# Filling TensorE's waits with products of the identity that nothing reads, in a two-layer perceiver block

## The reference, cut to what matters

```python
x = x + xattn0(layernorm(x), ctx)        # 16 heads, 4096 keys, relative bias
x = x + ssm(layernorm(x))                # projection in, convolution, selective scan, gate, projection out
x = x + mix(layernorm(x))                # token shift, r = sigmoid(xr Wr), k = relu(xk Wk)^2, r * (k Wv)
x = x + xattn1(layernorm(x), ctx, mask)  # 16 heads, 4096 keys, masked
x = x + tm(layernorm(x))                 # v, r, decay scan over time, projection out
x = x + ffn(layernorm(x))                # gate, up, down with rounded weights and activations
```

## Time and profile before

| | us |
|---|---|
| median of 3 runs | 1400.04 (1394.95, 1400.04, 1403.46) |
| the profiled execution | 1400.61 |
| its span in the trace | 1398.7 |
| PE busy | 1245.5 (89%) |
| DVE busy | 1027.9 (73%) |
| ACT busy | 928.2 (66%) |
| POOL busy | 203.0 (15%) |
| mean granted clock of TensorE | 0.929 |

### The profile page before, as it was taken

One profiled execution on the slowest core, in us unless ns is written; L12 is line 12 of the kernel. 1 busy time (PEld: TensorE's weight loads), 2 busy tenths in 40 slices (PEclk: granted clock), 3 DMA queues, 4 the chain that ended last, 5 costly groups with the idle time before them and its releaser, 6 DMA issues.

```text
span 1398.7 us, 25689 instructions
## 1 busy us (share of the span) xinstructions
PE 1245.5 (89%) x8951; PEld 647.6 (46%) x8952; DVE 1027.9 (73%) x2295; ACT 928.2 (66%) x1203; POOL 203.0 (15%) x183
## 2 busy tenths in 40 slices
PE   7759989999999999789998629999999999999746
PEld 4436634544454446345555411445445445445423
DVE  4217889999999971469999439878778787781666
ACT  2316757667767776356675181799999999999614
POOL 2212200000000000059996040000000000000000
PEclk9979989999999999999999765899999999999875
DMA  4898885455455310117776856134434344300000
GB/s 154 211 240 265 260 224 116 93 130 115 93 122 113 73 45 20 68 57 248 259 248 218 221 83 139 32 74 81 87 69 93 69 86 80 75 2 23 1 0 15
DMA packets 100684, 160.97 MB, mean 115 GB/s; under 512 B 8497, under 2 KB 57137, under 8 KB 100065
## 3 DMA queue, kind: packets, MB, share of 16 engines
q1 hardware_dynamic: 99088, 158.13, 46.1%
q10 hardware_dynamic: 1488, 1.42, 0.4%
HBM read 114.34 MB, written 45.18 MB: 114 GB/s over the span
## 4 chain that ended last, share of the span: by engine, by line
PE 64%; DVE 12%; issue 11%; ACT 5%; DMA 2%; SPq 2%; POOL 1%; DVEq 1%; POOLq 0%; ACTq 0%
PE PS L546 17%; PE PS L501 16%; PE PS L533 15%; PE PS L525 4%; PE PS L274 3%; PE PS L283 2%; DMA Pz<-in_ctxT 2%; ACT Pz L668 2%; DVE Vz L1068 2%; DVE OT L1076 2%; DVE Kz L1068 1%; PE PS L799 1%; ACT Pz L666 1%; SPq L262 1%; PE PS L858 1%
## 5 line engine op out<-in xcount | busy, mean ns | idle before, releaser
L668 ACT ACTIVATE Pz<-PS 128x1024 f32<-128x1024 f32 x488 | 483.5, 1018 | 125.8 <-PE PS L533 123.2
L589 DVE CUSTOM_DVE_ANT_0 Pz<-PS,Tz 128x512 bf16<-128x512 f32 x512 | 334.4, 689 | 88.4 <-PE PS L501 84.3
L501 PE MATMUL PS<-Kz,Qz 96*128 96x512 bf16 x1024 | 366.0, 401 | 32.3 <-issue 22.0
L533 PE MATMUL PS<-Qz,Kz 99*128 99x256 bf16 x2048 | 310.7, 274 | 4.7 <-ACT Pz L666 3.0
L586 DVE TENSOR_REDUCE mx<-PS 128x1 f32<-128x512 f32 x448 | 289.6, 686 | 14.2 <-PE PS L501 13.5
L546 PE MATMUL PS<-Pz,Vz 128*17 128x256 f32 x4096 | 272.4, 384 | 0.2 <-ACT Pz L668 0.2
L533 PEld LDWEIGHTS PS<-Qz,Kz 99*128 99x128 bf16 x2048 | 195.3, 98 | 124.9 <-ACT Pz L666 10.4
L501 PEld LDWEIGHTS PS<-Kz,Qz 96*128 96x128 bf16 x1024 | 99.5, 98 | 197.3 <-DVE mx L589 77.8
L546 PEld LDWEIGHTS PS<-Pz,Vz 128*17 128x17 f32 x4096 | 94.2, 97 | 133.0 <-issue 61.2
L672 ACT ACTIVATE PS<-Tz 128x512 f32<-128x512 bf16 x240 | 144.3, 601 | 7.6
L525 PE MATMUL PS<-Tz,identb 128*128 128x512 bf16 x272 | 105.0, 386 | 4.1 <-ACT Pz L668 3.9
(11 more groups left out here) (218 smaller groups left out, 1209.4 us busy)
## 6 DMA issues: line engine op xcount, KB each, us to landing
k_parts<-Pz SPq DMA_DIRECT2D x192, 128.0 KB
Kz<-k_parts SPq DMA_DIRECT2D x64, 384.0 KB, 4.8
v_ones<-Pz SPq DMA_DIRECT2D x32, 544.0 KB, 5.1
Vz<-v_ones SPq DMA_DIRECT2D x64, 272.0 KB, 6.0
Pz<-in_ctxT SPq DMA_DIRECT2D x32, 512.0 KB, 5.9
Kz<-k_parts SPq DMA_DIRECT2D x64, 256.0 KB, 5.5
Kz<-k_parts SPq DMA_DIRECT2D x64, 128.0 KB, 5.9
Kz<-in_mask_pieces SPq DMA_DIRECT2D x16, 512.0 KB, 5.8
```

The lines of the kernel that those rows point to most:

```text
L501: e.matmul(PS[:, unit_bank(k, u) if bank is None else bank, :], Qz[0:ROWS, o:o + 128], Kz[b][0:ROWS, hh, c * CH:c * CH + CH], start=True, ...
L533: m = e.matmul(PS[:, bank, o:o + T], Kz[b][0:KROWS, hh, i * 128:i * 128 + 128], Qz[0:KROWS, q:q + T], start=(L == 0), stop=True, skip_grou ...
L589: e.tensor_tensor_reduce(junk[:, u % 3, :], ps, masks[:, tt, c * CH:c * CH + CH], 1.0, LOWEST, ALU.add, ALU.max, to).then_inc(sem("at_seen ...
L668: m = e.activation(probs(i), PS[:, 2 * (i % 2):2 * (i % 2) + 2, :].rearrange("p a n -> p (a n)"), ACT.Exp)
```

## The change

A helper puts `n` products of the bf16 identity with itself (four times side by side, 512 columns) into one PSUM bank. Calls of it are put behind and between TensorE's work in the layer norms but the first, in `fin_pe`, behind the output projection of the state space step (with a wait for the value copies out of bank 6 ahead of it), in the mixing, in the fourth part and in the feed-forward's down part. No other engine's list changes, and no existing product, wait or increment.

```diff
+        def keep_busy(e, n, bank=6):
+            for _ in range(n):
+                e.matmul(PS[:, bank, :].rearrange("p (a n) -> p a n", n=128), identb[:, :],
+                         identb[:, :].unsqueeze(1).broadcast_to([128, 4, 128]), start=True, stop=True,
+                         skip_group_check=True)
 def ln_pe(e, k):
                     m = e.transpose(PS[:, c, r * 128:r * 128 + 128], xn[:, r, c * 128:c * 128 + 128], identf[:, :])
+                    if k and c == 0 and r < RT - 1:
+                        keep_busy(e, 1)
                 m.then_inc(sem("ln_tps"), 1)
+            if k:
+                keep_busy(e, 5)
 def fin_pe(e, L):
             fin_pe_sums(e, L, 4)
+            keep_busy(e, 3)
             fin_pe_spread(e, L, 4)
+            keep_busy(e, 4)
             for r in range(RT // 2, RT):
                 fin_pe_rows(e, L, NG - 1, r)
+            keep_busy(e, 14)
 def ssm_pe(e):
             proj_pe(e, lambda m_, r: yg[:, m_, r * 128:r * 128 + 128], wout, DC)
+            e.wait_ge(sem("kv_vcopied"), 8 * NCH + 2)
+            keep_busy(e, 16)
 def mix_pe(e):
             e.wait_ge(sem("ld_mix"), 16 * 4)
+            keep_busy(e, 18)
             e.wait_ge(sem("mix_x"), 2 * KC)
...
             proj_pe(e, lambda m_, r: ka[:, m_, r * 128:r * 128 + 128], wval, KC)
+            keep_busy(e, 21)
 def tm_pe(e):
                     m.then_inc(sem(name), 1)
+            keep_busy(e, 24)
             e.wait_ge(sem("tm_w"), 2)
             proj_pe(e, lambda m_, r: t1[:, m_, r * 128:r * 128 + 128], wout1, KC)
+            keep_busy(e, 42)
 def down(r):
                 s = r % 2
+                if r == 2:
+                    keep_busy(e, 8, 2)
+                if r == 3:
+                    keep_busy(e, 12, 2)
                 e.wait_ge(sem("ff_quant"), r + 2)
...
                 m.then_inc(sem("ff_htps"), 1)
+                if r >= 2:
+                    keep_busy(e, 4, 2)
                 e.wait_ge(sem("ff_hqT"), r + 1)
```

## The result

The changed kernel takes 1384.55 us (median of 14 runs, 1379.55 to 1392.80), the kernel before 1399.47 us (14 runs, 1393.15 to 1404.87). The ratio is 0.9902, with a 95% interval of 0.9879 to 0.9925: faster by 10.5 to 16.9 us, 13.7 in the middle; the medians lie 14.9 apart. The forecast was 1388.5, with 1381 to 1398.

What follows compares the result with a forecast made beforehand. A serial chain whose TensorE products run at half clock after idle waits bounds it. Gains of 13.4 us, less 0.36, 0.1 and 1.0, net 11.9: 1400.6 to 1388.7, stated as 1388.5 us, range 1381 to 1398.

Steps and rivals of the forecast that it cites:

- Half of the time at half clock comes back: Between and after the attentions: half of TensorE's chain time at half clock can be won, 13.4 us before losses.
- the up products: Feed-forward: some 5 us at half clock until 1370.4, gain between 0 and 2.5 us, taken as 1.1.
- 0.22 us each: Cost of each of 223 added products at full clock, 49 us of TensorE, nearly all beside other work.
- The fillings fit: Added products end within TensorE's long waits, such as 42 taking 9.2 of 10.90 us; 0.3 to 1.7 us stays open.
- the 5: Products behind a norm's transposes: 1.1 us against a 0.78 us wait, 0.12 us late in three of four norms, -0.36.
- the 4: Added products inside fin, with 3 others, against waits as the 0.90 us ahead of L799; -0.1 us allowed in first fin.
- The end loses 1 us: Feed-forward's down steps: added products start at half clock and delay transposes; net -1.0 us, between +0.5 and -7.
- the 8 ahead of the third step: Down part: 3.4 us at half clock against a 1.12 us wait; third step's transposes some 1.7 us late.
- Rival 1: Remaining rests, mostly 0.3 to 1.7 us, let the clock fall in places; 6 us gain left, 1394.5 us; chance 0.14.
- Rival 2: Second attention's start bound by key loads, not queries, so the two middle parts give nothing: 1393.3 us; chance 0.08.
- Rival 3: Added products don't hold the clock, each takes 0.43 us and fillings overrun: about 23 us slower, 1424; chance 0.08.
- Rival 4: Each added product costs 0.32 us, fillings overrun, some 10 of 12 us gone: 1398.5 us; chance 0.06.

Runs made afterwards that it cites:

- the middle alone: Changed kernel keeping only the fillings from the second part's projection to the second attention's queries: 1391.78 us, ratio 0.9950 to the kernel before.

## Why the prediction was right

The lengths of the stretches, each between two VectorE instructions that both kernels have, set against the terms of the sum:

| stretch (us) | before | after | difference | predicted |
|---|---|---|---|---|
| first fin: reciprocal to `xn` | 6.92 | 7.01 | +0.1 | +0.1 |
| norm and L885, to the convolution's products | 13.50 | 11.29 | -2.2 | -2.1 |
| norm, mixing, to the gated product | 19.08 | 16.39 | -2.7 | -2.6 |
| gated product to `xn`, with the 21 fillings beside it | 6.85 | 6.85 | 0 | 0 |
| norm and queries, to the cast | 9.69 | 7.54 | -2.1 | -2.0 |
| cast to the second attention's first reduction | 22.50 | 22.26 | -0.2 | 0 |
| second fin: reciprocal to `xn` | 8.20 | 7.26 | -0.9 | -0.95 |
| norm and L1223, to the scans | 10.58 | 8.08 | -2.5 | -2.3 |
| scans, L858, to `xn` | 16.77 | 15.37 | -1.4 | -1.45 |
| to the copy behind L1380 | 8.06 | 7.64 | -0.4 | -0.4 |
| up products, to the fourth tile's product | 17.00 | 15.28 | -1.7 | -1.1 |
| down part, to the last output | 14.94 | 15.81 | +0.9 | +1.0 |

The sum of the differences is -13.3 (-11.9 predicted; the ratio's interval gives 10.5 to 16.9). The medians lie 14.9 apart, and 12.6 by the ratio when the changed kernel was run again: what they have over or under the stretches is not shown to be more than chance. Point by point:

- *Half of the time at half clock comes back, the other engines' steps stay*: shown row by row. The one that was taken at a middle value, the up products, was the one most off: 1.7 for 1.1; the clock held through the wait ahead of them in both profiles of the changed kernel.
- *0.22 us each*: shown (42 in 9.23 us).
- *The fillings fit; the 5 and the 4 are a little late*: shown; fin is 0.1 longer, and the 5 end at the next product's start, without idle.
- *The end loses 1 us*: shown by taking the 28 products out, 14.9 for 15.8 us. The clock rose at 1369.8, within the 8 ahead of the third step, as the sum assumed, and those transposes came late.
- Rival 1, falls in the rests: none in the two profiles of the changed kernel. In the run with transposes and in the one with three more waits filled it came, at the place named, ahead of the up products, and cost 0.9 us in that stretch each time (16.15 for 15.27): little of the 6 us that the rival would take. With three more waits filled the unfilled down part behind it was shorter by as much (14.09 for 14.94), with transposes the filled one was longer (16.88). Rival 2, a transfer that doesn't move: fell by the middle alone; the stretch from the cast to the first reduction lies between 22.15 and 23.05 in all ten traces. Rival 3, products that hold nothing: fell; even transposes hold. Rival 4 fell with the 0.22 us.
- One reading was short: the earlier trace rows have the end at half clock for 21.5 us, not 19. No term of the sum rests on it.

Between the two profiled executions lie 17.5 us, 4.2 more than the table explains. 4.0 of them lie ahead of the first fin, where no edit is; there the two agree in code and differ by chance. Two unfilled waits moved against each other: L906 lost 1.7 us, the projection behind the scan won 1.1. Why a run of the untouched first part is some microseconds faster or slower was not looked into.

## What to carry to other kernels

In a serial chain of small products, read the granted clock in the same windows as the waits: here half of the time in which products on the chain ran at half clock was what could be won. Products or transposes that nothing reads held the clock; sized a wait at a time, from its idle time over 0.22 us, so that they end before the next operand is there, they cost next to nothing (0.1 us at the first fin). A quarter of their columns in the same places kept it in some waits only. Count them at the clock that will be there when they start: the 8 that started at half clock took 2.74 us, where 8 at 0.22 take 1.8, and the step behind them came late.

## What was not expected of the hardware

- Transposes of the identity kept the granted clock at 1.00 through 36 us (770.0 to 806.0), with plain products of the kernel between them, and through 9.5 us (1335.10 to 1344.60) in which TensorE ran only these, but for the end of one product.
- An idle of 3.11 us ahead of the same instruction left the clock at 1.00 in one execution (3.67 us for 8 products) and at half in the other (5.37 us): equal waits don't decide alike from run to run. In the eight traces in which this wait has no filling, the 8 products took 3.67 us three times and 5.33 to 6.52 five times; with the wait filled they took 3.67 both times. How much of the spread of some 12 us between runs of one kernel comes from such places is not shown.
